# A two-layer language-model tower on one core: masking first in the first attention, gathers spread over its steps, another order in the preparing steps and for the row maxima of the softmax attention

## The reference

```python
h = take(W.T, ids) + b + positional_encoding                    # [2, 2048, 128]
# first attention: 8 heads of 16, no softmax; a normalization over all earlier dots
x = layernorm(h); q, k, v = split(x @ w_qkv)
dots = where(causal, q @ k.T * dim ** -0.5, 0)
mu   = diagonal(cummean(dots)); t = dots - mu
s    = diagonal(cummean(t * t))
attn = where(causal, t * rsqrt(s + 1e-8) * norm_g + norm_b, 0)
h    = h + (attn @ v) @ w_out + b_out
# second part: 2 heads of 64, l2-normalized queries and keys, softmax; then 8 experts of 512
hx = layernorm2(layernorm(h)); q, k = l2norm(hx @ Wq) * scale * qn_g, l2norm(hx @ Wk) * scale * kn_g
y    = softmax(causal(q @ k.T * 64 ** -0.5)) @ (hx @ Wv) @ Wo
gate = softmax(y @ gate_W + gate_b)
h    = h + sum_e gate_e * (gelu(y @ W1_e + b1_e) @ W2_e + b2_e)
```

## Time and profile before

| | us |
|---|---|
| three runs | 933.99, 934.61, 935.84 (median 934.61) |
| profiled execution, own time | 937.37 |
| its span, first to last instruction | 935.5 |
| mean granted TensorE clock | 0.945 of full speed |
| busy: TensorE matmul, VectorE, ScalarE, GpSimd | 800.4, 681.4, 487.5, 327.0 |
| stages in the trace: first attention, preparing, softmax attention, experts | to 260, to 352, to 592, to 935 |

### The profile page before, as it was taken

The page is one execution under the profiler, slowest core; times in us unless marked ns, Lnnn a source line. Parts: engine busy times, 40 slices in busy tenths (PEclk is TensorE's granted clock), DMA queues, the critical chain, the costliest instruction groups (busy, mean ns, idle before and its releaser), DMA issues.

```text
span 935.5 us, 20835 instructions
## 1 busy us (share of the span) xinstructions
PE 800.4 (86%) x8228; PEld 563.9 (60%) x8228; DVE 681.4 (73%) x1547; ACT 487.5 (52%) x999; POOL 327.0 (35%) x371
## 2 busy tenths in 40 slices
PE   1683898889986676878889988999999999999997
PEld 0462677667753343545546555667777777777775
DVE  2643667776667765666565643789999999999997
ACT  0331454455434334566767889555555555555553
POOL 7456556665645433455555654000000000000000
PEclk9976999999978658999999999999999999999999
DMA  4111001010000000000000000000000000000000
GB/s 132 28 30 46 23 12 34 24 34 12 2 0 1 0 1 1 2 2 2 2 2 2 1 3 2 2 2 13 2 14 4 11 13 2 13 2 13 1 14 12
DMA packets 9488, 12.01 MB, mean 13 GB/s; under 512 B 1832, under 2 KB 6576, under 8 KB 9264
## 3 DMA queue, kind: packets, MB, share of 16 engines
q1 hardware_dynamic: 8368, 8.59, 3.1%
q0 software_dynamic: 1024, 2.10, 0.8%
HBM read 8.59 MB, written 2.10 MB: 11 GB/s over the span
## 4 chain that ended last, share of the span: by engine, by line
PE 69%; DVE 14%; ACT 6%; issue 5%; POOL 5%; DMA 0%; DVEq 0%; ACTq 0%; POOLq 0%
PE ps L928 67%; DVE mx L792 3%; ACT room L528 2%; POOL h_all L231 2%; DVE y L679 2%; POOL ss L324 2%; DVE room L883 1%; DVE qkn L746 1%; DVE x L725 1%; ACT room L527 1%; ACT room L403 1%; DVE room L659 1%; POOL sm L268 1%; DVE ss L731 1%; ACT room L389 1%
## 5 line engine op out<-in xcount | busy, mean ns | idle before, releaser
L543 ACT ACTIVATE cst<-ps,col 128x512 f32<-128x512 f32 x256 | 175.8, 688 | 163.1 <-PE ps L928 162.4
L928 PEld LDWEIGHTS ps<-arena,sq 128*128 128x128 f16 x3072 | 192.3, 98 | 61.6 <-DVE sq L912 3.5
L928 PE MATMUL ps<-arena,sq 128*128 128x128 f16 x3072 | 213.0, 219 | 0.7 <-DVE sq L912 0.7
L928 PE MATMUL ps<-y,arena 128*128 128x512 f16 x768 | 208.5, 381 | 1.3 <-DVE och L863 1.3
L912 DVE TENSOR_TENSOR sq<-cst,sq 128x512 f16<-128x512 f32 x256 | 175.8, 687 | 4.4
L355 POOL TENSOR_TENSOR room<-room 128x512 f16<-128x512 f32 (+3 forms) x111 | 112.9, 1030 | 109.0 <-ACT room L528 103.0
L792 DVE TENSOR_REDUCE mx<-ps 128x2 f32<-128x1024 f32 (+2 forms) x76 | 81.6, 1074 | 55.2 <-PE ps L928 55.2
L907 DVE CAST sq<-cst 128x512 f16<-128x512 f32 x256 | 108.9, 426 | 11.9 <-ACT cst L543 4.5
L527 ACT ACTIVATE room<-ps 128x512 f32<-128x512 f32 (+3 forms) x160 | 86.3, 539 | 47.2 <-PE ps L928 46.7
L528 ACT ACTIVATE room<-ps 128x512 f16<-128x512 f32 (+3 forms) x160 | 87.0, 544 | 0.0
L928 PEld LDWEIGHTS ps<-y,arena 128*128 128x128 f16 x768 | 64.9, 98 | 34.2 <-issue 3.7
(11 more groups left out here) (153 smaller groups left out, 1179.6 us busy)
## 6 DMA issues: line engine op xcount, KB each, us to landing
sq<-w_rows SPq DMA_DIRECT2D x16, 256.0 KB, 2.8
out<-h_all SPq DMA_DIRECT2D x32, 64.0 KB, 1.6
cst<-consts SPq DMA_DIRECT2D x1, 1294.0 KB
h_all<-emb_rows,idx POOLq DMA_INDIRECT x32
c<-consts SPq DMA_DIRECT2D x1, 256.0 KB
wqkv<-w_qkv SPq DMA_DIRECT2D x1, 192.0 KB
wsm<-w_sm SPq DMA_DIRECT2D x1, 192.0 KB
row<-rows SPq DMA_DIRECT2D x1, 140.0 KB
```

The lines of the kernel that those rows point to most:

```text
L543: a.activation(hid[:, f], ps[:, HBANK[f], :], ACT.Gelu_apprx_tanh, bias=col[:, K_B1 + k:K_B1 + k + 1], scale=1.0 / WS).then_inc(S["hid_rea ...
L928: return t_.matmul(o, l, r, start=start, stop=stop, skip_group_check=True)
```

## The change

On VectorE `masked(c, 0)` goes ahead of `variances(c-1)` in every step of the first attention, and in its first step `embed(1)` goes ahead of `normed(0)`. The gathers have one semaphore per step, for which `embed` waits; 4 are issued before the first `front`, 2 and 10 among the first duties, and then 2 in each of the steps 1 to 8. The weight pieces move from steps 1 to 13 to steps 4 to 13 (two each in steps 4, 5, 7, 9, 10, 12). The constants are loaded in two parts, of which the first (with two positional tiles) has a semaphore with the rows, and the token bias is added in two parts. Memsets move behind the first `front`. In the preparing steps VectorE does `normed2`, `sum_squares(c+1)`, `unit_qk(c)` in this order, TensorE does `project2` before `unit_T`, and the first block's row scores go one per step in steps 5 to 12, with their maxima one step later. In the softmax attention no step has three parts; the second part of a step is made behind `values` (on VectorE behind the low half), `max_row` moves to the step before the item's first one and ahead of `values`, and ScalarE copies its row between the exponentials of the two heads. The parts stand two in a step in steps 1 to 6, 9, 12, 15, 17, 20, 26, 31, 37 and 42.

```diff
@@ -178,6 +178,7 @@
         S = {name: sem(name) for name in names.split()}
+        GATHERED = [sem(f"gathered{c}") for c in range(NT)]
         NPIECE = 2 * E * FF // 512
@@ -189,7 +190,7 @@
         ds = bass.ds
-        WAT = {c: [n for n in range(NPIECE) if n * 13 // NPIECE + 1 == c] for c in range(NT)}
+        WAT = {c: [n for n in range(NPIECE) if n * 10 // NPIECE + 4 == c] for c in range(NT)}
@@ -197,9 +198,10 @@
             sp.dma_start(idx[:], ids).then_inc(S["load_c"], 16)
-            sp.dma_start(row[:], rows).then_inc(S["load_w"], 16)
-            sp.dma_start(cst[:], consts).then_inc(S["load_w"], 16)
+            sp.dma_start(row[:], rows).then_inc(S["load_a"], 16)
+            sp.dma_start(cst[:, 0:C_POS + 2 * D], consts[:, 0:C_POS + 2 * D]).then_inc(S["load_a"], 16)
             sp.dma_start(wqkv[:].rearrange("p a d -> p (a d)"), w_qkv).then_inc(S["load_w"], 16)
+            sp.dma_start(cst[:, C_POS + 2 * D:], consts[:, C_POS + 2 * D:]).then_inc(S["load_w"], 16)
             sp.dma_start(col[:], cols).then_inc(S["load_w"], 16)
@@ -230,21 +232,14 @@
                                          in_offset=bass.IndirectOffsetOnAxis(ap=idx[:, t:t + 1], axis=0)
-                                         ).then_inc(S["gathered0" if t < B else "gathered1" if t < 8 else "gathered"], 16)
+                                         ).then_inc(GATHERED[t // B], 16)
...
             g.memset(l2_eps, L2_EPS).then_inc(S["setup"], 1)
-            g.memset(v16[:, :, :, DS:DS + 1], 1.0).then_inc(S["setup"], 1)
-            g.memset(mpad[:], 0.0).then_inc(S["setup"], 1)
-            for i in range(2):
-                g.memset(kv[i][:, :, :, 2 * DA:2 * DA + 1], 1.0).then_inc(S["setup"], 1)
-                g.memset(kv[i][:, :, :, 2 * DA + 1:], 0.0).then_inc(S["setup"], 1)
-            g.memset(sg[:], 0.0).then_inc(S["setup"], 1)
-            gather(B, 9)
-            pool.wait_ge(S["setup"], 10)
-            pool.wait_ge(S["load_w"], 80)
+            gather(B, 2 * B)
+            pool.wait_ge(S["setup"], 3)
@@ -283,16 +278,22 @@
             front(0, 0)
-            gather(9, 13)
+            gather(4, 6)
+            for i in range(2):
+                g.memset(kv[i][:, :, :, 2 * DA:2 * DA + 1], 1.0).then_inc(S["setup"], 1)
+                g.memset(kv[i][:, :, :, 2 * DA + 1:], 0.0).then_inc(S["setup"], 1)
+            g.memset(sg[:], 0.0).then_inc(S["setup"], 1)
             front(1, 1)
-            gather(13, 18)
+            g.memset(v16[:, :, :, DS:DS + 1], 1.0).then_inc(S["setup"], 1)
+            g.memset(mpad[:], 0.0).then_inc(S["setup"], 1)
+            pool.wait_ge(S["setup"], 10)
+            pool.wait_ge(S["load_a"], 32)
             out_bias(0)
             out_bias(1)
-            gather(18, 22)
+            gather(6, 16)
             coefs(0)
...
             front(2, 0)
-            gather(22, 24)
@@ -302,11 +303,12 @@
                     out_bias(c + 1)
+                if 16 + 2 * c <= T:
+                    gather(14 + 2 * c, 16 + 2 * c)
                 for n in WAT[c]:
...
             step_a(1, 0, tail=False)
-            gather(24, T)
             for c in range(2, NT - 2, 2):
@@ -526,10 +528,10 @@
                         a.activation(phi[:, i % PR, lo:], ps[:, i % 3, lo:], ACT.Exp).then_inc(S["p_ready"], 1)
+                        if s in RAT and i == 2 * s:
+                            max_row(RAT[s])
                     if s < 2:
                         high_qk(NT - 2 + s)
-                if s in RAT:
-                    max_row(RAT[s])
                 for m in range(LAST):
@@ -553,14 +555,17 @@
                 v.memset(credit[:, i:i + 1], 0.0).then_inc(S[name], size)
-            dve.wait_ge(S["load_w"], 80)
-            v.tensor_scalar(qkg8[:], col[:, K_QG:K_QG + 1], float(DS) ** 0.5, None, ALU.mult).then_inc(S["pos_ready"], 1)
-            v.tensor_tensor(pos, pos, row[:, R_TB:R_TB + D].unsqueeze(1).to_broadcast([P, NT, D]),
-                            ALU.add).then_inc(S["pos_ready"], 1)
-            dve.wait_ge(S["pos_ready"], 2)
+            def token_bias(c0, c1):
+                v.tensor_tensor(pos[:, c0:c1], pos[:, c0:c1], row[:, R_TB:R_TB + D].unsqueeze(1).to_broadcast([P, c1 - c0, D]),
+                                ALU.add).then_inc(S["pos_ready"], 1)
+
+            dve.wait_ge(S["load_a"], 32)
+            token_bias(0, 2)
+            dve.wait_ge(S["pos_ready"], 1)
...
                 h = h_all[:, ds(2 * c, 2), :]
+                dve.wait_ge(GATHERED[c], 16 * B)
                 v.tensor_tensor(h, h, cst[:, ds(C_POS + c * D, D)].unsqueeze(1).to_broadcast([P, B, D]),
@@ -598,17 +603,19 @@
-            dve.wait_ge(S["gathered0"], 16 * B)
             embed(0, 0)
+            embed(1, 1)
             normed(0, 0)
-            dve.wait_ge(S["gathered1"], 16 * (8 - B))
-            embed(1, 1)
             dve.wait_ge(S["xn0_sb"], 1)
...
             normed(1, 1)
+            dve.wait_ge(S["load_w"], 64)
+            v.tensor_scalar(qkg8[:], col[:, K_QG:K_QG + 1], float(DS) ** 0.5, None, ALU.mult).then_inc(S["pos_ready"], 1)
+            token_bias(2, NT)
+            dve.wait_ge(S["pos_ready"], 3)
             links = 0
@@ -681,9 +688,9 @@
                 cur = 1 - nxt
+                masked(c, 0)
                 if not first:
                     variances(c - 1, nxt)
-                masked(c, 0)
                 state_out(c, 0)
@@ -697,7 +704,6 @@
             step_a(1, 0, first=True)
-            dve.wait_ge(S["gathered"], 16 * (T - 8))
             for c in range(2, NT - 2, 2):
@@ -757,8 +763,8 @@
+            masked(NT - 2, 0)
             variances(NT - 3, 1)
-            masked(NT - 2, 0)
             state_out(NT - 2, 0)
@@ -769,8 +775,8 @@
             h1_out(NT - 3)
+            masked(NT - 1, 0)
             variances(NT - 2, 0)
-            masked(NT - 1, 0)
             dve.wait_ge(S["wlow_ready"], NPIECE)
@@ -798,16 +804,20 @@
+            def single_max(i):
+                r, h = i // HS, i % HS
+                row_max(0, r, 0, (r + 1) * P, i, (h,))
+
             def step_b(c):
-                unit_qk(c)
                 if c + 2 < NT:
                     normed2(c + 2)
+                if c + 1 < NT:
+                    sum_squares(c + 1)
+                unit_qk(c)
+                if 0 <= c - 6 < 8:
+                    single_max(c - 6)
                 if c:
                     low_qk(c - 1)
-                if c + 1 < NT:
-                    sum_squares(c + 1)
-                if 0 <= c - 9 < 4:
-                    row_max(0, c - 9, 0, (c - 8) * P, 2 * (c - 9) + 1, (1,))
                 if c == 3:
@@ -821,14 +831,12 @@
                     outputs(NT - 1, 1)
-                if 0 <= c - 8 < 4:
-                    row_max(0, c - 8, 0, (c - 7) * P, 2 * (c - 8), (0,))
...
                 step_b(c)
+            sum_squares(NT - 1)
             unit_qk(NT - 2)
             low_qk(NT - 3)
-            sum_squares(NT - 1)
             low_v(NT - 1)
@@ -867,7 +875,7 @@
                     low_qk(NT - 2)
-                for part in MSLOT.get(s, ()):
+                for part in MSLOT.get(s, ())[:1]:
                     row_max(*part, (0, 1))
@@ -882,6 +890,8 @@
                                         ).then_inc(S["plo_dve"], 1)
+                for part in MSLOT.get(s, ())[1:]:
+                    row_max(*part, (0, 1))
                 for m in range(LAST):
@@ -984,9 +994,9 @@
-            pe.wait_ge(S["load_w"], 80)
-            pe.wait_ge(S["setup"], 10)
+            pe.wait_ge(S["load_a"], 32)
             xn_T(0, 0, first=True)
+            pe.wait_ge(S["load_w"], 64)
             project(0, 0, first=True)
@@ -996,6 +1006,7 @@
             xn_T(1, 1, first=True)
+            pe.wait_ge(S["setup"], 10)
             sums(0, 0, 0, first=True)
@@ -1113,19 +1124,17 @@
                     normed_T(c + 2)
-                if 0 <= c - 9 < 4:
-                    row_scores(c - 9, 1)
-                unit_T(c)
                 if c + 2 < NT:
                     project2(c + 2)
+                unit_T(c)
                 if c == 1:
...
                     out_project(NT - 1)
-                if 0 <= c - 8 < 4:
-                    row_scores(c - 8, 0)
+                if 0 <= c - 5 < 8:
+                    row_scores((c - 5) // HS, (c - 5) % HS)
@@ -1275,12 +1284,14 @@
                     unit_T(NT - 2 + s)
-                for part in MSLOT.get(s, ()):
+                for part in MSLOT.get(s, ())[:1]:
                     pair_scores(*part)
+                if s in RAT:
+                    max_row(RAT[s])
                 if LAG <= s < NSTEP + LAG:
                     values(s - LAG)
-                if s in RAT:
-                    max_row(RAT[s])
+                for part in MSLOT.get(s, ())[1:]:
+                    pair_scores(*part)
                 for m in range(LAST):
@@ -1340,18 +1351,19 @@
                     k += 1
-    due = [None, 2] + [f - 3 for f in first[2:]]
+    due = [None, 2, 6] + [f - 3 for f in first[3:]]
```

(13 more changed lines are left out.)

2 lines of the change are left out of this document (1 added, 1 removed).

## The result

The changed kernel takes 919.28 us, median of 4 runs (916.65 to 922.03), against 934.3 for the kernel before beside it: ratio 0.9835, 95% interval 0.9806 to 0.9864. The prediction was 886.0 with a range of 871 to 902. The sign was right and the size was not: 15 us came of 48.

What follows compares the result with a forecast made beforehand. TensorE was taken to bound the first attention, a loop of engine waits the preparing steps, TensorE's row-maxima waits the softmax attention. Gains 7 + 18.2 + 8.7 + 4.5 + 10 = 48.4 from 937.4: 889.0, median 886, range 871 to 902.

Steps and rivals of the forecast that it cites:

- The stall: First attention, step 2: VectorE's idle wait for the last gather goes, with the eight late gathers; gain 18.2 us.
- The start: Ahead of the first `front`: fewer gathers, shorter token bias and moved memsets gain 7 us, bounds 5 and 8.5.
- Mask first: First attention, steps 3 to 14: mask ahead of variances removes TensorE's 1.35 us hole, 16.2 us gross, steps net 8.7.
- the collision: First attention: VectorE's variances are held up beside GpSimd's weight pieces and lose 6.9 us in sum.
- rival 1: First attention: variances slip between GpSimd's weight pieces undisturbed, so the steps gain 15.6 us; 879 us, chance 0.15.
- Preparing steps: Preparing stage: sums of squares ahead of `unit_qk` and spread row scores remove waits; gain 4.5 us, bounds -5 and +8.
- Rival 2: Preparing steps stay at TensorE's lower clock, a loss of 5 us instead of a gain of 4.5; 896 us, chance 0.2.
- sums of squares first: Preparing steps: `sum_squares(c+1)` ahead of `unit_qk(c)` on VectorE makes GpSimd's factors a step ahead; the 0.82 us wait goes.
- Softmax attention: Softmax attention: second parts behind `values` save 12 of 26.1 us of waits, `max_row` loses 2; gain 10, bounds 3 and 17.
- Rival 3: First attention becomes limited by GpSimd, outputs late, period 13.3 us again, 8.7 lost; 895 us, chance 0.15.
- rivals 4: First attention: an early wait of `embed` on its gather brings back most of the stall, 15 us; 901 us, chance 0.04.
- 5: First attention: GpSimd and VectorE take turns entirely, about 16.4 us a step, so the kernel is slower; 938 us, chance 0.02.

Runs made afterwards that it cites:

- Experiments 7: Changed kernel with the preparing steps' order undone (903.21 us), plus the big loads issued only once the first two gathers have landed: 905.73 us.
- 10: Changed kernel with the preparing steps' order undone (903.21 us), plus big loads held until four gathers have landed and `normed(0)` ahead of `embed(1)`: 898.63 us.
- experiment 3: Changed kernel with VectorE's variances ahead of the first mask again in all steps of the first attention: 923.46 us.
- experiment 12: Changed kernel with `unit_T` ahead of `project2` on TensorE and `unit_qk` ahead of norms and sums of squares on VectorE, both as before the change: 904.36 us.

## Why the prediction was right and wrong

- **The stall: right.** 18.2 us said, 18.2 found (step 2 from 30.15 to 11.91; a clean step 11.91 where the prediction had 11.98).
- **The start: right in kind, 2.3 us off.** The bound of 5 "where the fourth gather lands behind the constants" is what came (4.7; the first matmul at 14.19 us, where 12 was to be the sign). Experiments 7 and 10 show it was the gathers' landing beside the big load and what follows it, the first gathers as well as the fourth, together with `embed(1)` ahead of `normed(0)`. Part of the size is chance: with one and the same start, the first dots of step 1 came anywhere from 47.7 to 50.5 us.
- **Mask first and the collision: net 6.5 for 8.7.** Two sizes and a wait behind it were off. The hole of 1.35 us was taken as wholly the order's; experiment 3 shows 0.51 us of it in a step without pieces. The clean step came out as forecast only because mask first and the later pieces together remove the hole; that is luck, since the prediction gave it all to the order. And the collision was put at 6.9 us over the ten steps, 1.1 in one with two pieces and gathers; against 11.91 it came to 10.4, 1.6 to 1.8 in such a step. The step that failed is "L659 waits 0.5 for the first, the two-input instructions behind it for the second": L666, the same instruction, did not slip through between the two pieces, and took 2.21 to 2.42 us in three of the six steps with two. With it failed "State and embedding lie between and fit": the sum looked only at `out_T`, and TensorE's larger wait was for the state, 0.89 us against 0.27. L666 takes 0.42 us in all 15 places once the pieces are off GpSimd, so rival 1 (no collision) is out. By the Trainium skill (SBUF — State Buffer, Who interferes with whom), a VectorE instruction with two SBUF inputs and a GpSimd instruction that reads SBUF keep each other out. The trace agrees beside the pieces, and the hold was longer than one GpSimd instruction; it doesn't agree beside GpSimd's power, where such an instruction (L569) took its usual 0.41 us.
- **Preparing steps: wrong, 16.6 us, half of the miss.** The sentence that failed is "`unit_T` no longer fills TensorE's wait for ScalarE", which followed `unit_T` no further. It releases `high_qk(c)`, and that stands in ScalarE's queue ahead of `squares(c+2)` and `normed_T(c+3)`. With `unit_T` behind `project2(c+2)` the ring is not the 5.0 us of the sum (`normed2`, the transposed input, projection and squares) but, from start to start in the chain above, 2.90 + 0.87 + 0.39 + 0.47 + 0.48 + 0.27 + 0.47 + 0.68 = 6.53. Rival 2 had the direction and the lower clock, and a loss of 5 for 12.1. The stage took 87.9 us, past the 80 that the prediction itself had named as proof against it. The arithmetic slipped too: two thirds of 65 + 4 and a third of 77 + 4 make 73.0 and not 71.3, a gain of 2.8 and not 4.5. The gain on the other side, sums of squares first, was nothing (experiment 12): TensorE waits for VectorE by one name or the other.
- **Softmax attention: wrong, 10.5 us.** The step that failed is "I count 12 saved of 26.1". The mechanism was there, and too small: the waits between the parts fell by 4.6 us (20.4 to 15.8), and those ahead of `max_row` grew by 2.8 where 2 had been forecast, so the sum fell from 26.1 us only to 24.3, not to 16. By the runs the part is worth 1.7 to 3.7 us, clock included, where 10 had been forecast; why the changed kernel's own stage was 0.5 us longer than before stays open, within the 4 us by which this stage differs between traces of the same code.
- Rival 3 (GpSimd as the limit, 13.3 in all steps) did not come: steps with pieces took 12.2 to 13.7 us, those without 11.91, and in step 5 GpSimd was idle 1.4 us ahead of its power (L263). Nor did rivals 4 and 5: VectorE waited for no gather from step 1 on, and the kernel is faster.

## What to carry to other kernels

When an instruction is moved behind another on one engine, follow what it releases into the queue of the next engine, and on round until the ring closes: the item it releases may stand ahead of what the ring itself needs. GpSimd's subtractions for the weights held up VectorE's variances here wherever the two met; they were best given to VectorE, in a wait that VectorE had anyway, and were faster there too. In this kernel the first gathers were only as early as the loads beside them allowed, and a wait removed in an in-order queue is worth only the distance to the next wait in it.

## What the runs showed of the hardware

- An operation of VectorE with two SBUF inputs (L666) that started during GpSimd's first piece did not get in between two pieces that followed without a gap: 2.21 us for 0.42, to the end of both. Beside GpSimd's power over 16 elements (2.94 us long) the same kind of operation (L569, 0.41) was not held.
- Two gathers issued by 5.2 us had landed at 10.8 us (9.9 to 11.1 in the other traces with these loads) with 1.3 MB of constants and some 0.9 MB of other loads issued by about the same time, and by 6.9 us with 0.9 MB of the constants and the 0.5 MB issued behind them held back.
- Step 1 of the first attention took 13.0 to 13.1 us in ten traces, with a granted clock of 0.88 or 0.89, and 14.4 to 14.5 us in seven, with 0.79 or 0.80 (one more: 13.9 us at 0.84). With the same start, the first dots of step 1 came at 47.7 to 50.5 us. Executions thus differ by 2 to 3 us before the steps begin, and one profile can't tell smaller gains.
